# Layer-norm transposes drained by VectorE, gate matmuls issued in half batches, mask loads paced by five

## The reference, cut

```python
xn = _layernorm(x, axis=-1)                          # [8, 2048, 4096]
# masked linear: a 32x32 block of weight counts only if its mask block has a one
bm = mask.reshape(Nb, 32, Kb, 32).sum(axis=(1, 3)) > 0
attn = einsum('bsk,nk->bsn', xn, weight * bm_expanded) + bias
# linear with 8 gated low-rank experts
q = xn @ Wq.T ; k = xn @ Wk.T                        # 8 experts x 32
w = softmax(sum(q * k, -1) / sqrt(32))               # per token, over experts
h = xn @ A.T                                         # 8 experts x rank 16
ffn = xn @ W.T + b + einsum('bse,bser,eor->bso', w, h, Bm)
out = x + attn + ffn
```

## Time and profile before

| | us |
|---|---|
| median of 2 runs | 2494.06 (2493.5 to 2494.62) |
| the profiled execution, its own time | 2496.06 |
| its span, slowest core (core 6; all cores 2473.9 to 2494.2) | 2494.2 |

### The profile page before, as it was taken

The page is one execution under the profiler, slowest core; times in us unless marked ns, Lnnn a source line. Parts: engine busy times, 40 slices in busy tenths (PEclk is TensorE's granted clock), DMA queues, the critical chain, the costliest instruction groups (busy, mean ns, idle before and its releaser), DMA issues.

```text
span 2494.2 us, 24302 instructions; the slowest of 8 cores (2473.9 to 2494.2 us)
## 1 busy us (share of the span) xinstructions
PE 2123.4 (85%) x10092; PEld 997.1 (40%) x10092; DVE 470.8 (19%) x583; ACT 320.0 (13%) x472; POOL 144.5 (6%) x237
## 2 busy tenths in 40 slices
PE   0235764653999999999999999999999999999999
PEld 0122321221444444444444444444444444444444
DVE  1443456522111111111111111111111111111110
ACT  4784621110000000000000000000000000000000
POOL 1102222200000000000000000000000000000000
PEclk9997777675999999999999999999999999999999
DMA  7758999914233333333333333333333323333331
GB/s 148 185 155 151 179 158 175 173 36 95 64 72 68 68 68 68 68 68 68 68 68 68 72 80 81 82 88 72 68 68 68 68 68 68 68 68 68 68 71 48
DMA packets 227037, 220.88 MB, mean 89 GB/s; under 512 B 34160, under 2 KB 185840, under 8 KB 226800
## 3 DMA queue, kind: packets, MB, share of 16 engines
q0 software_dynamic: 57104, 106.97, 25.5%
q1 hardware_dynamic: 169824, 112.36, 15.7%
HBM read 292.69 MB, written 33.55 MB: 131 GB/s over the span
## 4 chain that ended last, share of the span: by engine, by line
PE 73%; ACT 1%; DMA 1%; issue 0%; DVEq 0%; ACTq 0%; POOL 0%; DVE 0%; POOLq 0%
PE ACC L718 71%; ACT stuff L742 1%; PE T_ps L653 1%; PE ACC L727 1%; DMA WT_ring<-WTb 1%; DVEq L660 0%; POOL wm_ring L665 0%; ACTq L740 0%; ACTq L33 0%; DVE out_sb L697 0%; DVEq L33 0%; DVEq L695 0%; DVEq L694 0%; POOLq L621 0%
## 5 line engine op out<-in xcount | busy, mean ns | idle before, releaser
L718 PE MATMUL ACC<-xn_fm,wm_ring 128*128 128x512 bf16 x4096 | 1219.1, 379 | 20.3 <-DMA WT_ring<-WTb 20.3
L718 PE MATMUL ACC<-xn_fm,WT_ring 128*128 128x512 bf16 x4096 | 1219.0, 379 | 0.0
L718 PEld LDWEIGHTS ACC<-xn_fm,wm_ring 128*128 128x128 bf16 x4096 | 400.9, 98 | 497.0 <-issue 21.4
L718 PEld LDWEIGHTS ACC<-xn_fm,WT_ring 128*128 128x128 bf16 x4096 | 401.0, 98 | 483.9 <-issue 1.1
L697 DVE TENSOR_TENSOR out_sb<-T_ps,x_res 128x512 f32<-128x512 f32 x128 | 82.5, 686 | 1494.8 <-PE T_ps L653 1494.8
L742 ACT ACTIVATE stuff<-ACC,biassum 128x1024 f32<-128x1024 f32 x64 | 71.3, 1114 | 1776.4 <-PE ACC L727 1776.4
L328 PE MATMUL gen_ps<-xn_fm,genring 128*128 128x512 bf16 x640 | 187.5, 459 | 81.2 <-ACT genring L411 78.5
L358 PE MATMUL XT_ps<-idbf_sb,xn_tm 128*128 128x128 bf16 x512 | 58.2, 292 | 191.5 <-DVE xn_tm L301 151.1
L256 DVE TENSOR_REDUCE S1k<-mk_st 128x32 bf16<-128x1024 bf16 x128 | 153.7, 1216 | 125.0 <-DMA mk_st<-mask 124.4
L683 DVE TENSOR_TENSOR wm_ring<-wm_ring,bmE_pT 128x4096 bf16<-128x4096 bf16 x32 | 141.6, 4426 | 182.6 <-DMA wm_ring<-wTb 182.6
L328 PEld LDWEIGHTS gen_ps<-xn_fm,genring 128*128 128x128 bf16 x640 | 69.5, 112 | 196.0 <-issue 150.2
(11 more groups left out here) (64 smaller groups left out, 203.6 us busy)
## 6 DMA issues: line engine op xcount, KB each, us to landing
x_t<-x SPq DMA_DIRECT2D x64, 512.0 KB, 7.1
mk_st<-mask POOLq DMA_DIRECT2D x128, 256.0 KB, 7.7
x_res<-x SPq DMA_DIRECT2D x64, 512.0 KB, 7.8
wm_ring<-wTb POOLq DMA_DIRECT2D x32, 1024.0 KB, 8.7
WT_ring<-WTb POOLq DMA_DIRECT2D x32, 1024.0 KB, 13.8
out<-out_sb SPq DMA_DIRECT2D x128, 256.0 KB, 13.3
genst<-qkhTb SPq DMA_DIRECT2D x40, 256.0 KB, 8.7
genring<-qkhTb POOLq DMA_DIRECT2D x40, 128.0 KB, 6.4
```

Of the source, the lines that this page charges most:

```text
L718: mm = t.matmul(ACC[th].ap()[:, j * 512:(j + 1) * 512], ring.ap()[:, sl * D + kc * 128:sl * D + (kc + 1) * 128], xn_fm.ap()[:, kc * T + th ...
```

## The change

- The drains of `XT_ps` move from ScalarE to VectorE. `emit_xnev` and its calls are gone; VectorE gets four `tensor_copy` for each tile, behind that tile's four applies and ahead of its three mask reductions.
- From tile 8 on, TensorE issues the gate matmuls as 20 behind the second chunk's transposes and 20 behind the fourth's, where it issued 40 behind the fourth's.
- In the slice loop of GpSimd's queue a mask load follows slice u when `u % 5 < 3` (21 loads over slices 5 to 39), where it followed unless `u % 4 == 0` (27 loads).

```diff
@@ GpSimd's queue
         for u in (range(5, NGS) if DO_S1 else []):
             emit_slice(u)
-            emit_mask(g, 0 if u % 4 == 0 else 1)
+            emit_mask(g, 1 if u % 5 < 3 else 0)
         emit_mask(g, NMQ)
-
-    def emit_xnev(s, u):
-        s.wait_ge(S["l_xt"], u + 1)
-        s.activation(
-            xn_fm.ap().rearrange("p (kc t) -> p kc t", t=T)
-                [:, 8 * (u % 4):8 * (u % 4) + 8, (u // 4) * 128:(u // 4 + 1) * 128],
-            XT_ps[u % 2].ap().rearrange("p (a b) -> p a b", a=8),
-            AF.Identity, bias=0.0, scale=1.0,
-        ).then_inc(S["l_xev"], 1)
@@ ScalarE
                 s.activation(xsq.ap(), xa, AF.Square,
                              accum_out=st(sl, 4 + qq)).then_inc(S["l_xq"], 1)
-                if ti >= 1:
-                    emit_xnev(s, 4 * (ti - 1) + qq)
@@
             .then_inc(S["l_sq"], 1)
-        for qq in range(4):
-            emit_xnev(s, 60 + qq)
@@ VectorE, behind the applies of tile ti
+            for qq in range(4):
+                u = 4 * ti + qq
+                v.wait_ge(S["l_xt"], u + 1)
+                kc0 = 8 * qq
+                v.tensor_copy(
+                    xn_fm.ap().rearrange("p (kc t) -> p kc t", t=T)
+                        [:, kc0:kc0 + 8, ti * 128:(ti + 1) * 128],
+                    XT_ps[u % 2].ap().rearrange("p (a b) -> p a b", a=8),
+                ).then_inc(S["l_xev"], 1)
             if DO_MASK:
                 for _ in range(3):
                     emit_reduce(v, mrq[0])
@@ TensorE, in the loop over qq
                 mm.then_inc(S["l_xt"], 1)
-            if ti >= 8:
-                if ti == 8:
-                    t.wait_ge(S["l_xev"], 32)
-                emit_th0(40)
+                if ti >= 8 and qq % 2 == 1:
+                    if ti == 8 and qq == 1:
+                        t.wait_ge(S["l_xev"], 32)
+                    emit_th0(20)
```

## The result

The changed kernel is slower: 2507.99 us median of 17 runs against 2494.55 of 16 runs of the kernel before, a ratio of 1.0049 with a 95% interval of 1.0036 to 1.0062, some 12 us. (In some executions the cores of a die run at a lower clock; the medians include those, the ratios here leave them out, and of the profiled executions only that of drains_only was such a one.) The profiled execution of after has a span of 2502.6 us on its slowest core, core 2. The forecast was 2481, range 2469 to 2497. What came is rival C, whose price was 2503; how much of that is luck is told under the rivals.

A forecast was written before the change was run, and what follows sets the result against it. Main-block matmuls were taken as the rigid bound, so only time won before the gate matmuls end at 512 us counts. 22 - 4 - 5 = 13 us won, from 2494.06 to 2481 us, range 2469 to 2497.

The forecast's parts named there:

- rival C: Slower: every tile from 8 on waits for its own third mask to land; 24.4 us a tile, 2503 us; chance 0.2.
- the gain in tiles 0 to 7: Drains moved to VectorE shorten most tiles from 15.6 to 12.7 us, winning 22 us by the applies of tile 8.
- the landing of the masks in tiles 8 to 15: Third mask load of each tile, from issue to its reduction: taken as 6 us, from tile 9 of before.
- What bounds the kernel: Main-block matmuls, 71% of the span, stay rigid; only the end of the gate matmuls at 512 us can move.
- x is no new wait: Tiles 0 to 7: x loads are released by the applies as before, so they add no wait.
- Rival B: VectorE's drain copies run at one column a cycle, 1.2 us each: 6 us won, 2488 us; chance 0.12.
- The ring: Tiles 8 to 15: each waits on its own third mask's issue, landing and reduction; 21.3 us a tile, 4 us lost.
- DMA has less to do per tile than before: Tiles 8 to 15: mask landing should be nearer to tile 9's DMA share of 0.86 than to 1.14.
- The end of the layer norm: Tile 15: VectorE drains behind 20 matmuls before reducing, with the mask ring full; 5 us lost (0 to 8).
- Its threshold: Slower case takes over above 23.4 us a tile from tile 8 on, a mask landing of 8.1 us.
- D: Faster: x is early, masks land in 4.5 us from tile 8 on; tiles of 19 to 20 us, 2470; chance 0.15.
- E: No change: time won ahead of the DMA-bound stream after tile 15 is lost in it; 2492 to 2495 us; chance 0.08.

The follow-up runs named there:

- drains_only: The changed kernel with one batch of 40 gate matmuls and the old mask order, so only the drains stay moved: 2472.75 us, ratio 0.9892.
- thin_x: The changed kernel loading only the first 256 of each 1024 columns of x from tile 9 on: 2486.0 us, ratio 0.9982.
- last_mid: The changed kernel with tile 15's three mask reductions put between its drains 1 and 2: 2498.77 us, ratio 1.0034.
- no_split: The changed kernel with its gate matmuls in one batch of 40, new mask order kept: 2505.5 us, ratio 1.0042.
- lead29: The changed kernel with 29 mask loads in front of the slice loop instead of 24, new order kept: 2465.48 us, ratio 0.9889.

## Why the prediction was wrong, step by step

Two terms of the sum failed: the gain in tiles 0 to 7, because x became a new wait (15.9 won for 22), and the landing of the masks in tiles 8 to 15 (19.3 lost for 4). Together they are 21 us of the 25 between a forecast of 13 won and some 12 lost; the rest lies between the stages and the total and is not explained. Both had been named as signs of being wrong: ScalarE waiting for x, and tiles above 23.4 us.

**What bounds the kernel** held: the main block took 1885.5 us, and what happened in the tiles came out at the end.

**Tiles 0 to 7, forecast 22 won: 15.9.** VectorE's side was right to a tenth; the other side was not. After, core 2, the tile that begins at 112.68:

```profile
112.68 2.98 DVE L288 TENSOR_SCALAR xn_tm<-x_t,stats 128x1024 bf16<-128x1024 f32 x4 [0.18 <-DVE stats L283]
...
118.38 0.69 DVE L298 COPY xn_fm<-XT_ps 128x1024 bf16<-128x1024 bf16 x1 [0.16 <-PE XT_ps L354]
118.99 3.46 DVE L243 TENSOR_REDUCE S1k<-mk_st 128x32 bf16<-128x1024 bf16 x3
119.71 1.06 ACT L221 ACTIVATE xsq<-x_t 128x1024 bf16<-128x1024 f32 x1 [2.65 <-DMA x_t<-x]
...
124.48 0.19 ACT L226 ACTIVATE stats<-stats 128x1 f32<-128x1 f32 x1
```

Copy 3 ends at 6.4 us and the reductions at 9.8 behind the applies, as worked out. But the sum goes off at 11.8, not 9.9: ScalarE waits 2.65 us for the third chunk of x. "x is no new wait" was the failed step. The loads are released by the applies as before, but ScalarE, 2 us quicker through its first two chunks, now comes for the third before it has landed. Core 2 waits 11.6 us for x between 57 and 154 us, in eight waits of up to 2.7 us. The mean of the cores, from the applies of tile 1 to those of tile 8, is 11.4 us in after and 1.0 in before. A part of each wait reaches the end of its tile, and I put the missing 6 us down to them. No run took these waits away by themselves. The Trainium skill's estimate for the copy ("VectorE: DVE Perf Modes", section on the errata), 0.66 us at 2x, agrees with the 0.686 measured. Rival B, copies at one column a cycle, fell with that number. The row in "Rules for kernel authors" that the prediction set beside B gives two ways, to accept 1x or to copy to SBUF first, and it gives no time for such a copy; so it did not speak for B's 1.2 us.

**Tiles 8 to 15, forecast 4 lost: 19.3.** The ring was the right one. This is tile 9 of after, core 2:

```profile
176.83 2.98 DVE L288 TENSOR_SCALAR xn_tm<-x_t,stats 128x1024 bf16<-128x1024 f32 x4 [0.18 <-DVE stats L283]
...
183.70 0.55 POOL L176 DMA_DIRECT2D mk_st<-mask  x1
...
188.04 0.55 POOL L176 DMA_DIRECT2D mk_st<-mask  x1
...
193.29 1.22 DVE L243 TENSOR_REDUCE S1k<-mk_st 128x32 bf16<-128x1024 bf16 x1 [6.44 <-DMA mk_st<-mask]
...
198.01 1.22 DVE L243 TENSOR_REDUCE S1k<-mk_st 128x32 bf16<-128x1024 bf16 x1 [0.78 <-DMA mk_st<-mask]
```

The third mask load was issued 11.2 us after the applies (forecast 11.4). It was reduced 10.0 us later, not 6 (188.04 to 198.01). That is the term that was mis-sized, by 4 us in this tile, one of the longest: 25.34 us against 21.3. Over the tiles 8 to 14 and all cores the third mask was issued at 11.7 us, reduced 8.0 later, and the next applies came 3.9 behind: 23.6 us, so the landing term was 2.0 us short on the mean, 14 us in seven tiles. The issue came within 0.3 us of the forecast, so neither the matmuls nor their clock made the difference. I had taken 6 from tile 9 of before, whose loads go out from 11.6 us behind the applies on the earlier trace rows; its last chunk of x had landed at 9.9. The new kernel issues the first at 6.9 us, with two chunks of x still under way (the last landed at 10.1), and its eight slice and mask loads then land one behind the other until 22.6. thin_x took most of x away: 5.5 us to landing, and 21.0 us a tile. So "DMA has less to do per tile than before, so landing should be nearer to tile 9's" was the wrong inference: the mean share says 0.78, but the mask loads now start before the x loads have ended.

There was also a question that I did not ask. I compared the new ring with the 20.9 us mean of before, and took the lead of the old order as worth little more than it had earned there. In a kernel with the drains moved the old order gives 130.2 us, and 29 in front gives 122.5. The right comparison was with what the other two edits would have earned with masks in hand. Asking it would not have changed the forecast of the time, but it would have shown that the third edit was the one to doubt.

**The end of the layer norm, forecast 5 lost (0 to 8): 5.3.** Right in place and size; last_mid takes 7.2 us off that stage, and no_split, where VectorE does not wait for a batch before its last drains, 6.9.

**The rivals.** C came true in its mechanism: every tile from 8 on waits for the landing of its own third mask. It stood at 0.2. That its 2503 is within 5 us of the measured 2508 is in part luck: it had 26 us lost in the tiles, where 19.3 were, and 22 won before them, where 15.9 were, and the two errors cancel. Its threshold was off for the same reason. With 15.9 won and 5.3 lost behind, a tile of 22.4 us breaks even, not 23.4; at 23.6 C's own sum would have given no more than 1 or 2 us lost. Of the two rows that spoke for it, the 9.1 us was measured at a higher DMA share, and I took that as a reason to discount it. The 26.26 us of tile 8 did not speak for a long landing at all: over the cores of before that tile's third mask was issued at 15.3 us and reduced 6.7 later. But nothing except tile 9 spoke for 6 us either. D's tile of 19 to 20 us was there too (18.6 with the old order, and 2469 us in all), and what it took was the old order. E, that time won ahead of the DMA-bound stream is lost in it, is refuted: lead29 wins 14.3 + 23.5 us in the tiles and gives back 3.1 behind them.

## What to carry to other kernels

When an edit makes a supply exactly match the use (three loads a tile for three reductions a tile), ask what is in hand at the start: with nothing in hand, each tile here became a chain of issue, landing and use (11.7 + 8.0 + 3.9 us), and no engine looked busy. A landing time taken from a trace holds for the moment in the tile at which that transfer was issued; if the edit moves the issue, look at what else is in flight at the new moment. And where a bundle of edits is to be judged, ask of each what it does once the others have worked: here two were worth 25 us together, and the third, one line, cost some 39.

## What was not expected of the hardware

The landing time of a 256 KB mask load went from 5.5 to 8.1 us (medians of 200 to 300 us) with three quarters of the x traffic put back, at a mean DMA share of only about 0.8 (core 6 of thin_x and core 2 of after). Over all cores the medians are 5.5 and 7.6. The share of 200 to 300 us in after, core 2, in 40 slices of 2.5 us (tenths, 9 being 90% or more):

```profile
DMA  0269899990039999996026999995008999999410
```

The mean is 0.77, but the DMA engines go from nearly nothing to 90% and more within each tile, and the mask loads fall into the full part. So a mean share well below one did not mean that a transfer was alone.
